# A decoder's product-key retrieval: half of the private state moved into the weighting stage, and casts moved to ScalarE

## The reference, cut to what matters

```python
h = act(jnp.einsum('btd,cd->btc', hidden_states, W_up) + b_up)      # 256 -> 1024, silu
h = jnp.einsum('btc,pc->btp', h, W_down) + b_down                   # -> 128, "private state"
q = jnp.einsum('btp,rp->btr', h, W_q)
sim = jnp.einsum('pbthn,hkpn->pbthk', q, keys)                      # 2 sides, 8 heads, 45 keys
scores, idx = lax.top_k(sim, K_PER_HEAD)
...
sc, pk = lax.top_k(all_scores, K_PER_HEAD)                          # best 8 of 8 x 8 sums
de, ue = down_embed[indices], up_embed[indices]
z = act(jnp.einsum('btd,bthkd->bthk', h, de) * jax.nn.softmax(sc, axis=-1))
out = jnp.einsum('bthk,bthkd->btd', z, ue)
```

## Time and profile before

| | |
|---|---|
| median of 3 runs | 984.23 us (982.48 to 991.62) |
| the profiled execution | 986.36 us, of which the span of the trace is 984.5 |
| mean granted clock of TensorE in it | 0.889 |
| busy: TensorE, VectorE, ScalarE, GpSimd | 775.3, 733.8, 557.0, 564.2 us |

### The profile page before, as it was taken

How to read it: one execution, slowest core, us unless ns; L and a number is a source line. 1 busy time by engine, 2 the same in 40 slices (tenths; PEclk the granted TensorE clock), 3 DMA queues, 4 the chain that set the end, 5 groups by cost and what they waited for, 6 DMA issues and landing times. The chain is left out here.

```text
span 984.5 us, 14033 instructions
## 1 busy us (share of the span) xinstructions
PE 775.3 (79%) x4673; PEld 498.4 (51%) x4673; DVE 733.8 (75%) x1291; ACT 557.0 (57%) x1028; POOL 564.2 (57%) x440
## 2 busy tenths in 40 slices
PE   4999989847777877778779988767777777789991
PEld 2554754425656666666664366623333333356551
DVE  4766258189999999999962755789999999354564
ACT  2314113278778687687751454678888888214440
POOL 3115200198999999999941032257777776215642
PEclk9999999979999879889999989977777767779996
DMA  5002030000000000000006000979999999222224
GB/s 176 1 0 86 1 107 29 0 1 1 0 1 1 1 1 1 0 1 1 1 1 220 11 1 1 285 143 184 187 174 172 171 162 184 61 73 75 81 72 160
DMA packets 149525, 69.61 MB, mean 71 GB/s; under 512 B 139003, under 2 KB 144909, under 8 KB 148302
## 3 DMA queue, kind: packets, MB, share of 16 engines
q1 hardware_dynamic: 147150, 62.42, 29.0%
q0 software_dynamic: 2304, 6.29, 2.2%
HBM read 27.46 MB, written 7.68 MB: 36 GB/s over the span
## 5 line engine op out<-in xcount | busy, mean ns | idle before, releaser
L750 POOL TENSOR_TENSOR r_pairs<-r_side_exp 128x945 f32<-128x945 f32 x128 | 225.4, 1805 | 0.0
L853 ACT ACTIVATE r_w<-r_w,r_scale 128x1001 f32<-128x1001 f32 (+1 forms) x128 | 144.9, 1135 | 72.4 <-DVE r_w L938 57.6
L1722 ACT ACTIVATE c_probs<-c_scores,c_bias,c_q_scale 128x1024 int16<-128x1024 f32 x128 | 154.2, 1204 | 30.5 <-DVE c_bias L1735 21.7
L804 PE MATMUL r_head_sum<-ident,r_w 128*128 128x128 f32 (+1 forms) x1024 | 136.2, 293 | 43.2 <-ACT ctxT L864 21.8
L1659 POOL CAST kv_parts<-c_probs 128x1024 bf16<-128x1024 int16 x128 | 132.4, 1041 | 54.8 <-ACT c_probs L1722 53.8
L1733 DVE TENSOR_REDUCE c_neg_max<-c_scores 128x1 f32<-128x1024 f32 x128 | 155.5, 1215 | 6.5 <-PE c_scores L1672 6.3
L804 PEld LDWEIGHTS r_head_sum<-ident,r_w 128*128 128x128 f32 (+1 forms) x1024 | 125.8, 154 | 61.6 <-issue 34.8
L1672 PE MATMUL c_scores<-c_kT,c_placed 128*128 128x512 bf16 x256 | 105.1, 505 | 51.6 <-ACT c_probs L1722 48.1
L930 DVE SCALAR_TENSOR_TENSOR r_chosen<-r_pairs,r_kept,r_z 128x1024 f32<-128x1024 f32 (+1 forms) x104 | 128.0, 1272 | 4.4 <-ACT r_pairs L843 2.5
L938 DVE TENSOR_TENSOR r_w<-r_pairs,r_chosen 128x1024 f32<-128x1024 f32 (+1 forms) x104 | 121.3, 1204 | 0.0
L780 PE MATMUL r_head_sum<-r_up,ctxT 128*128 128x256 f32 x224 | 62.7, 449 | 21.8 <-ACT ctxT L864 21.8
(11 more groups left out here) (332 smaller groups left out, 1494.1 us busy)
## 6 DMA issues: line engine op xcount, KB each, us to landing
en_w<-in_w SPq DMA_DIRECT2D x1, 2992.0 KB, 12.1
ew_w<-in_w SPq DMA_DIRECT2D x1, 2992.0 KB, 12.2
ew_w_near<-in_w_near SPq DMA_DIRECT2D x1, 2176.0 KB, 21.8
r_up<-in_up SPq DMA_DIRECT2D x1, 2048.0 KB, 9.9
c_pT<-kv_parts SPq DMA_TRANSPOSE x128, 3.3
token_rows<-e_xn SPq DMA_DIRECT2D x2, 1024.0 KB, 5.8
e_row<-pick_rows SPq DMA_DIRECT2D x8, 256.0 KB, 4.4
zero_rows<-b_zeros SPq DMA_DIRECT2D x1, 1360.0 KB, 14.9
```

The costliest lines, as they stand in the source:

```text
L750: nc.gpsimd.tensor_tensor(pairs[:, v % MADE, BY_ACT * KEYS:].rearrange("p (a b) -> p a b", b=KEYS), a.broadcast_to([P, ROWS - BY_ACT, KEYS ...
L804: last = nc.tensor.matmul(head_sum[0:m, b // 4, (b % 4) * P:(b % 4 + 1) * P], w[:, v % RING, b * P:b * P + m], ident[:, :], start=(h == 0 ...
L853: nc.scalar.activation(w[:, v % RING, 0:COLS[f]], w[:, v % RING, 0:COLS[f]], ACT.Silu, scale=scale[:, t % 2, h:h + 1]).then_inc(silu_done, 1)
L1722: nc.scalar.activation(probs[:, u % RING, :], scores[:, u % SCORED, :, :].rearrange("p a b -> p (a b)"), ACT.Exp, bias=bias[:, t, h:h + 1] ...
```

## The change

- **`private_state` does only tokens 0 to 511**: 8 groups, one down-projection. ScalarE, and no longer VectorE, copies `to_sims` and makes `hT`. ScalarE also makes the four casts of `quantise_context`, one behind each of the last two Silus and two behind the copy of `to_sims`. VectorE does each step of it for both halves before the next.
- **The other 512 tokens are done in `weigh_experts`.** TensorE makes the scores of tiles 0 to 3 and projection 0, then the 8 groups into the two banks of `head_sum`, then the down-projection with projection 1 before its last two chunks, then the scores of tiles 4 to 7, also in `head_sum`. Only then do its transposes begin. ScalarE has the 8 Silus and the private state's bias among its rows and Silus of parts 0 to 6, and the score copies of tiles 4 to 7 at parts 6, 7, 8 and 8. The last of them and the rows of part 14 stand ahead of the Silu of part 8.
- **Projection 2** is issued before the transposes of part 3 instead of part 11. The first two copies of sums move from parts 8 and 16 to 14 and 18.
- **Memory**: the up weights lie in the last two slots of `pairs`, the down weights in the last slot of `w`, and `wide` in four slots before it. So parts 8 and 9 wait for the last group, and the weights' results from part 9 on for the last down-projection. `scale` lies in the unused end of the down table. VectorE's first pick waits for four score copies instead of eight.

Its core:

```diff
@@ private_state @@
-            for n, (c, h) in enumerate(groups):
-                if n == len(groups) - 2:
+            for c in range(UC):
+                if c == UC - 1:
...
-            pe.wait_ge(silu_ready, len(groups))
-            pe.wait_ge(copied, 1)
-            for h in range(NH):
-                for c in range(UC):
-                    last = nc.tensor.matmul(low[:, h, :], w_down[:, c, :], wide[:, c, h * HALF:(h + 1) * HALF],
-                                            start=(c == 0), stop=(c == UC - 1))
-                last.then_inc(low_ready, 1)
+            pe.wait_ge(pw.silu_ready, UC)
+            pe.wait_ge(pw.copied, 1)
+            for c in range(UC):
+                last = nc.tensor.matmul(low[:, 0, :], pw.w_down[:, c, :], wide[:, c, :], start=(c == 0), stop=(c == UC - 1))
+            last.then_inc(pw.low_ready, 1)
...
+                if c >= UC - 2:
+                    cast_context(nc, act, sh.cw, sh.kv, c - (UC - 2))
+            act.wait_ge(sims_ready, 1)
+            nc.scalar.copy(r.to_sims[:, :].rearrange("p (s n) -> p s n", s=2), low[:, :, 0:SIDE]).then_inc(pw.copied, 1)
+            for n in range(2, 4):
+                cast_context(nc, act, sh.cw, sh.kv, n)
+            act.wait_ge(pw.low_ready, 1)
+            nc.scalar.activation(r.hT[:, 0:HALF], low[:, 0, :], ACT.Identity, bias=pw.b_down[:, 0:1]).then_inc(pw.copied, 1)
@@ weigh_experts, TensorE @@
+                if t == SIMS_EARLY:
+                    projections(0)
+                    for c in range(UC):
+                        if c >= 2:
+                            pe.wait_ge(pw.silu_ready, UC + c - 1)
+                        private_up(nc, pw, c, head_sum[:, c % 2, :], xT[:, :, HALF:])
+                    pe.wait_ge(pw.silu_ready, 2 * UC)
+                    for c in range(UC):
+                        if c == PROJECT_IN:
+                            projections(1)
+                        last = nc.tensor.matmul(head_sum[:, 0, :], pw.w_down[:, c, :], wide[:, c, :], start=(c == 0), stop=(c == UC - 1))
+                    last.then_inc(pw.low_ready, 1)
+                    pe.wait_ge(pw.copied, 1 + NH)
+                if t > SIMS_EARLY:
+                    pe.wait_ge(sims_copied, t)
...
+            pe.wait_ge(sims_copied, NT)
             for v in range(PARTS_R):
                 k, t, f, h = place(v)
-                if h == PROJECT_AT[f] and k + 1 < HALVES:
+                if v == PROJECT_SOON:
+                    projections(2)
+                if h == PROJECT_AT[f] and 2 <= k < HALVES - 1:
                     projections(k + 1)
@@ weigh_experts, ScalarE (SILU_IN 1: 0 and 1, 3: 2, 4: 3; SILU_AT 0: 4, 1: 6; LOW_AT 6; SUMS_LATER 14: 0, 18: 1) @@
+            for t in range(SIMS_EARLY):
+                copy_sims(t)
             exps(0)
-            for t in range(2, NT):
-                copy_sims(t)
             for v in range(AHEAD):
                 first_rows(v)
+                for c in SILU_IN.get(v, ()):
+                    private_silu(c)
             for v in range(PARTS_R):
                 k, t, f, h = place(v)
+                if v == LOW_AT:
+                    private_low()
+                if LOW_AT <= v <= HEADS_R:
+                    copy_sims(SIMS_EARLY + v - LOW_AT)
                 if f == 1 and h == EXP_AT and t + 1 < NT:
                     exps(t + 1)
+                if v == HEADS_R:
+                    copy_sims(NT - 1)
+                    first_rows(v + AHEAD)
                 silu(v)
+                if v in SILU_AT:
+                    private_silu(SILU_AT[v])
-                if v + AHEAD < PARTS_R:
+                if v + AHEAD < PARTS_R and v != HEADS_R:
                     first_rows(v + AHEAD)
+                if v in SILU_AT:
+                    private_silu(SILU_AT[v] + 1)
+                if v in SUMS_LATER:
+                    copy_sums(SUMS_LATER[v])
-                if h == SUM_AT[f] and k >= 1:
+                if h == SUM_AT[f] and k - 1 >= len(SUMS_LATER):
                     copy_sums(k - 1)
@@ quantise_context @@
+def cast_context(nc, act, cw, kv, n):
+
+    r, half = divmod(n, 2)
+    at, rows, part = context_halves(cw, kv)[half]
+    act.wait_ge(kv.left, n + 1)
+    nc.scalar.copy(part(r), rows).then_inc(kv.cast, 1)
...
+    for at, rows, part in halves:
+        nc.vector.tensor_tensor(rows, rows, by_head(cw.scale, at), ALU.mult).then_inc(kv.left, 1)
+    for r in range(2):
+        for half, (at, rows, part) in enumerate(halves):
+            dve.wait_ge(kv.cast, 2 * r + half + 1)
+            last = nc.vector.tensor_tensor(rows if r == 0 else part(2), rows, part(r), ALU.subtract)
+            last.then_inc(kv.left if r == 0 else kv.split, 1)
```

More of the change, by code:

```diff
@@ L562, in load_private, with private_up @@
         sp.dma_start(dst, i[src]).then_inc(pw.loaded, 16)
+def private_up(nc, pw, c, to, tokens):
+    for d in range(DC):
+        last = nc.tensor.matmul(to, pw.w_up[:, d, c * P:(c + 1) * P], tokens[:, d, :], start=(d == 0), stop=(d == DC - 1))
+    last.then_inc(pw.up_ready, 1)
 def private_state(nc, sh, r, i):
@@ L577, in private_state @@
         loaded = pw.loaded
[L578 to L582, removed]
+        zeroed = sem("zeroed")
+        sims_ready = sem("sims_ready")
         block = ctx.enter_context(nc.Block())
@@ L693, in place, with sims_bank, pair_slot, w_slot @@
             return k, t, f, h
+        def sims_bank(t, s):
+            return chosen[:, t % 2, s, 0:SIDE] if t < SIMS_EARLY else head_sum[:, s, 0:SIDE]
+        def pair_slot(v):
+            n = v % MADE
+            return pairs[:, n, :] if n < MADE - 2 else pw.late_pairs[:, n - (MADE - 2), :]
+        def w_slot(v):
+            n = v % RING
+            return w[:, n, :] if n < RING - 1 else pw.late_w[:, :]
         def products(v):
             f = place(v)[2]
[L698 removed]
+            return pair_slot(v)[:, SKIP[f]:SKIP[f] + COLS[f]]
         def by_pool(v):
@@ new lines, in quantise_context @@
+    halves = context_halves(cw, kv)
+    for at, rows, part in halves:
+        last = nc.vector.tensor_tensor(cw.k[:, at, :], cw.k[:, at, :], cw.b_k[:, :].rearrange("p (o d) -> p o d", o=1).broadcast_to([P, NT // 2, D]),
+                                       ALU.add)
+    chain.step(last)
+    head_scales(nc, chain, cw.k, slice(0, NT), cw.scale, cw.inverse)
+    for at, rows, part in halves:
+        last = nc.vector.tensor_tensor(rows, rows, by_head(cw.inverse, at), ALU.mult)
+    chain.step(last)
@@ new lines, in quantise_context @@
+    for at, rows, part in halves:
+        last = nc.vector.tensor_scalar(cw.k[:, at, :], cw.k[:, at, :], ROUND, ROUND, ALU.add, ALU.subtract)
+    chain.step(last)
+    for at, rows, part in halves:
+        last = nc.vector.tensor_scalar(cw.k[:, at, :], cw.k[:, at, :], LEVELS, -LEVELS, ALU.min, ALU.max)
+    chain.step(last)
+    for at, rows, part in halves:
+        nc.vector.tensor_tensor(rows, rows, by_head(cw.scale, at), ALU.mult).then_inc(kv.left, 1)
[4 more added lines that the diff above has]
+            last.then_inc(kv.left if r == 0 else kv.split, 1)
```

128 lines of the change are left out of this document (62 added, 66 removed).

## The result

The changed kernel takes 974.9 us, median of 4 runs (974.09 to 979.93), against 986.89 for the kernel before (4 runs, 982.48 to 991.62): ratio 0.989, 95% interval 0.9853 to 0.9926. Against the median on which the prediction was made, 984.2, it is 9.3 us less; forecast were 974.5 us and 9.8 us. Against the median of all four runs before it is 12.0 less. The profiled span fell from 984.5 to 972.3.

A forecast was written before the change was run, and what follows sets the result against it. VectorE bounds the weighting, TensorE paces private_state before it. From 984.2 us, -16.6 - 1.0 + 3.1 + 3.2 + 1.5 = -9.8 gives 974.4, stated as 974.5; range 968.5 to 980.5.

The forecast's parts named there:

- Private state: private_state with only the first 512 tokens: VectorE's quantising ends it at 171.8, the weighting starts 16.6 us sooner.
- Start: From S, TensorE's start of the weighting block, to VectorE's first pick: S+13.05 instead of S+14.07, 1.0 us sooner.
- First pick to part 16: Second 512 tokens inside the weighting: VectorE waits 4.75 us in all, this length grows by 3.1 us.
- First residual: VectorE waits 3.9 us for TensorE's first output product instead of 0.63, so 3.2 us later.
- the clock: TensorE's clock may fall to 1.2 GHz behind new idle gaps: 1.5 us added, between 0 and 2.8.
- the third gap: TensorE's idle of 2.6 us ahead of projection 2; a clock fall there puts 1.5 us on the transposes.
- Behind it: After the first residual: the backlog is gone, projection 3 waits for pick 23 as before, no further wait moves.
- (a): Rival: cheaper hand-over, full clock, casts as short as VectorE's, half of 6.3 us of new waits absent; 969 us, chance 0.19.
- (b): Rival: dearer hand-over, casts near 2.3 us or both clock falls with delayed score round trips; about 979 us, chance 0.30.
- (c): Rival: TensorE stays at 1.2 GHz through the weighting's backlog, VectorE waits 24 us; 994.6 us, chance 0.03.
- (d): Rival: VectorE's quantising ends private_state, so the stage isn't shortened; 984 us, chance 0.03.
- The table load: ScalarE's table load before the exponential and rows of part 15: 1.28 us, without the skill's further 1.38 drain.

The follow-up runs named there:

- e3: Changed kernel with the two rows of part 15 made beside those of part 14, ahead of the table load and Silus of parts 8 and 9; ratio 0.9899 to before.
- e8: Changed kernel with the rows of part 14 back behind the Silu of part 8, the score copy's place kept; ratio 0.9899 to the kernel before.
- e4: Changed kernel with projection 2 before the transposes of part 6 instead of part 3; ratio 0.9892 to the kernel before.
- f1: Changed kernel with e1, e3 and e6 together and the first copy of sums behind part 13; 982.17 us, ratio 0.9813 to the kernel before.
- e1: Changed kernel with the four casts of the context's keys back on VectorE; ratio 0.9894 to the kernel before.
- e5: Changed kernel with the first residual alone after parts 22 and 23 instead of 20 and 21; ratio 0.9868 to the kernel before.
- f3: f1 with the casts left on ScalarE; 982.82 us, ratio 0.9832 to the kernel before.
- f2: f1 with the first tile's exponential moved ahead of the fourth score copy; 978.79 us, ratio 0.9788 to the kernel before.
- e6: e5 with projection 3 issued behind the first output product, ahead of part 16's transposes; ratio 0.9898 to the kernel before.
- e7: Changed kernel with projection 2 back before the transposes of part 11, copies of sums kept at parts 14 and 18; ratio 1.0008 to the kernel before.
- after_again: The changed kernel once more, unedited, on the chip of f1 to f3; 989.33 us, ratio 0.9896 to the kernel before.

## Why the prediction was right, point by point

- **Private state**: -16.6 forecast, -17.1 measured from the first up-projection on. VectorE ends it, as said, at 170.56 instead of 171.8: the cast was 1.03 instead of 1.1, and the first up-projection began 0.8 sooner, which belongs to no term.
- **Start**: -1.0 forecast, -1.4 measured. The fourth score copy ended at S+5.9 instead of 6.15, and the table load and exponential followed it at once.
- **First pick to part 16**: +3.1 forecast, +3.4 measured. Single waits were 0.3, 1.0, 0.75, 2.7 forecast and 0.42, 0.94, 0.69, 2.65 measured. All but the first wait for ScalarE's rows, as said, that of part 13 too. e3 and e8 show that the rows of 15 are what decides.
- **First residual**: +3.2 and +1.5 for the clock forecast, 4.7 together; +4.3 measured. The clock fell behind the third gap, ahead of projection 2, and cost 1.5 on the projection; it didn't fall behind the second, ahead of S. e3, e4 and f1 show that filling that gap moves the fall. The mark itself moves by 1.2 with the clock (e1), so +4.3 is one draw.
- **Behind it**: "no further wait moves" held in length, but e5 shows the wait for projection 3 right behind the residual's. It was hidden, not absent. Another 1.1 us was lost up to the last residual, which the sum had at nothing; 0.85 of it is the wait in the last tile. That wait is 12.6 to 13.0 in seven traces and 13.8 in the other seven, without regard to the edits, so no run ties it to the change.
- **The rivals**: (a) didn't come, since the waits are of ScalarE's order and all there. (b)'s dear casts didn't come; of its two clock falls one came in the changed kernel's trace. In e5 to e8 and in f3 one came behind the first gap and cost nothing. (c): TensorE didn't stay at the lower clock over the backlog, 40 transposes took 4.56 as at the full clock. (d)'s mechanism, quantising as the end of the block, is real, and was in the sum; f2 against f3 prices it at 2.7.
- **The table load**: 1.28, and the exponential starts at 178.07, 0.02 behind its end at 178.05, with its input long ready. ScalarE's copy ahead of the load starts at 176.00 and ends at 176.76. So the whole switch takes 1.31. By the rule of the Trainium skill (ScalarE: Activation LUTs, What ACT_TABLE_LOAD costs) it takes 2.66, of which 1.38 is a drain; the measurement decides against it here.

The mechanism was right at each step. The closeness of the sum, -9.8 for -9.6, is luck: its terms were off by 0.3 to 0.5 each with both signs, and one of 1.1 was missing. The closeness of the median, 974.9 for 974.5, is luck too: the span lost another 2.6 us where nothing was changed, the fourth run of the kernel before moved its median by 2.7, and single runs of the changed kernel lie between 974.1 and 979.9.

## What to carry to other kernels

Work moved under another stage takes its cover along: quantising cost nothing under 16 groups of matmuls and ended the block under 8. Where several engines' queues are interleaved by hand, a wait that is removed shows the next one behind it, so follow the chain to its end (rows of 15, copy of sums, output product, residual, projection 3) and move all its links together; e3, e4 and e5 alone moved the last residual by -1.5, +0.3 and -3.8 us, where the same code scatters by 2.1; f1, f2 and f3 moved it by -6.9, -7.5 and -7.1. Judge such edits by marks in the trace counted from a common event, not by medians whose intervals are 0.3% and more to either side, and learn first how far each mark repeats without an edit. Where the profile names the engine that ended a wait, check that its work was that part's: at part 13 it wasn't.

## What the runs showed of the hardware

- **The scatter of this kernel before the weighting goes with TensorE's clock.** In e1, e6, e7, e8 and f1 the first up-projection starts at 146.5 to 147.3, in all others at 142.3 to 143.3. Here is TensorE in the stretch 62 to 106 us of the changed kernel and of e8 (busy, instructions; granted clock; DMA share; GB/s):

```profile
62.00:78.00 16.00, 13.61 (x58) 1.00 0.24 81
78.00:106.00 28.00, 26.90 (x64) 1.00 0.08 30
```

```profile
62.00:78.00 16.00, 13.84 (x55) 0.92 0.19 66
78.00:106.00 28.00, 28.00 (x64) 0.93 0.10 38
```

  The program up to there is the same, and the mean clock 1.00 in one and 0.92 or 0.93 in the other. The same 64 matmuls from 77 or 79 us on take 27.63 in one and 29.30 in the other. By the first up-projection e8 is 3.9 us later.
- **The clock came back while TensorE did nothing but transposes.** In e3, over the 40 transposes at 227.80, the granted clock is 0.63 to 231.0, 0.81 to 233.8 and then 1.00.
- **The chips differ, and mainly in one part of the program.** The kernel before takes 985.89 and 986.12 us on the chips of e1 to e4 and e5 to e8, and 999.25 on that of f1 to f3 and `after_again`. `after_again` took 986.9 us of span against 972.3. Its VectorE in the weighting's last residual:

```profile
510.14 0.42 DVE L1009 TENSOR_TENSOR x<-x,r_z 128x256 f32<-128x256 f32 x1 [13.83 <-PE r_z L803]
```

  In the first profile that instruction starts at 510.05, so all but 0.1 of the 14.6 us lies behind it, in the stages that move most of the kernel's bytes. The other traces agree: from the last residual to the end of the span, the four of that chip take 476.4 to 478.0 and the eight of the other two 461.9 to 471.1. Which wait there takes it was not tested.
